# Cross-attention in split fp32: three waits at the two ends taken out, and ScalarE issuing the low query copies of every pair

## The chip, the cores and the metric

The kernel runs on one core of a Trainium2 chip. The metric is the device time of the whole program in microseconds (us), as the median of several executions. One further execution was recorded by the hardware profiler, and every duration below comes from it. The engines are named as in the profile: PE (TensorE, matrix products), PEld (its weight loads), ACT (ScalarE), DVE (VectorE), POOL (GpSimd) and SP (SyncE, which here only issues DMAs). A DMA is issued by an instruction in the queue of SP or ACT, and that queue goes on only when the issue is done; the page does not count this time as busy time of the engine. In the timelines such an issue stands under SPq or ACTq.

## The reference

Sixteen batches, 512 query rows of width 512, 77 context rows, 16 heads of width 32:

```
Q = split_heads(query @ Wq + bq)
K = split_heads(key @ Wk + bk)
V = split_heads(value @ Wv + bv)
scores = jnp.einsum('bhqd,bhkd->bhqk', Q, K) / np.sqrt(D_K).astype(np.float32)
attn = jax.nn.softmax(scores, axis=-1)
ctx = jnp.einsum('bhqk,bhkd->bhqd', attn, V)
ctx = ctx.transpose(0, 2, 1, 3).reshape(B, S, D_MODEL)
out = ctx @ Wo + bo
return _layer_norm(out + query, ln_gamma, ln_beta)
```

Key and value are both the context. All is float32.

## The kernel before

**Split operands.** A float32 product is made of three fast ones: each operand is split into a high part (rounded, by ACT) and a low part (the rest, by DVE or POOL), and high x high, high x low and low x high are summed in PSUM. So `xh`/`xl` are the query rows, `qh`/`ql` the projected queries, `ch`/`cl` the attention output, `woh`/`wol` the output weights.

**Stages.** `project_context` computes K for all batches (written to DRAM) and the first two row tiles of V. `attend` then runs 64 *slots*, one for each chunk of four heads of each batch, and four more to drain. In slot g the engines work on different chunks at once (the `LAG_` constants): PE projects the queries of chunk g into `p_q`, computes the scores of chunk g-3, multiplies probabilities with V for two chunks at a time in every odd slot, projects one 128-row tile of output (chunk number g-8) into `p_o`, and computes a first score pass `p_a` from which DVE takes row maxima. Slots go in *pairs* (2p, 2p+1), since `qh`, `ql`, the maxima `nmt` and the operand `z` of the scores are held for a pair, in two buffers.

**The operand z.** For the scores, `z` holds per head the high part of the query twice, the low part once and the row maximum, stacked on partitions. It is put together by DMAs from SBUF to SBUF: 8 copies of `qh`, 4 of `ql` (32 partitions by 1024 numbers each, one per head), 4 of `nmt`. SP issues all of them in the odd slot and the even one after it; only for the first pair and the last (`at_edge`) does ACT issue the four `ql` copies (`copy_low`), and SP the maxima right behind `qh`.

**Order.** Every engine runs its own list of instructions in program order, `slot(g)` for each g in turn (slots 16 to 55 in a hardware loop over eight slots). Waits are on semaphores. On ACT an odd slot ends with the exponentials `exp`, `ctx_high`, `mean_over_std`, `normalize`, then `split_x_high` (the high part of the query rows for five slots on) and `load_xt` (the next rows' DMA); the next even slot begins with `q_high`, which PE's `rowmax_scores` needs, then `ctx_high` and `exp`. POOL makes `xl` from `xh` (L1201) as the last step of a slot and, first thing in an even slot, two `cl` (L1220). PE's `project_out` needs the `cl` of chunk kc before it uses it, in the first tile of each batch, which falls in every fourth slot (`t == 0`, L733 to L735).

**The head.** In slots 2 to 9 the rest of V is projected in the place of `project_out`: PE writes `p_o`, DVE adds the bias (`add_bv`, L1079), ACT stores it. In slots 4 and 5 the four chunks of Wo are split by ACT (`woh`, L900) and POOL (`wol`, L1260); the raw chunks borrow buffers that DVE's `spread` and `divide` need afterwards. At the start of slot 8 ACT issues the DMAs of two residual tiles and of the rows `bo`, `ln_gamma` and `ln_beta`.

Of the kernel before, what the change touches and what calls it, by code (L numbers as in the profile page):

```python
# [26 lines left out]
P = 128  # L27
D = 512
KC = D // P
# [5 lines left out]
PAIR = 2 * NCH  # L35
# [325 lines left out]
def attend(nc, block, a, keep, kh_dram, kl_dram, v_dram, out, B, S, S2):  # L361
# [21 lines left out]
    with ExitStack() as ctx:  # L383
# [42 lines left out]
        stored = [sem(f"stored{i}") for i in range(4)]  # L426
        rows_in = sem("rows_in")
        x_last_in = [sem(f"x_last_in{t}") for t in range(QT)]
# [57 lines left out]
        def at_edge(g):  # L486

            return isinstance(g.u, int) and PAIR * g.u + g.k in (1, NG - 1)

# [36 lines left out]
        def _(sp):  # L526
# [63 lines left out]
            def slot(g):  # L590
                if g.k % 2 == 0 and g.back(2).valid(NG) and not at_edge(g.back(1)):
                    load_maxima(g.back(2))
                if g.k % NCH == 0 and g.valid(NG):
                    load_ks(g)
                if g.k % NCH == 2 and g.valid(NG):
                    load_v(g.back(2))
                if g.k % NCH == 2 and g.back(2 - NCH).valid(NG):
                    if g.back(2).is_first():
                        sp.wait_ge(kb1_zeroed, 1)
                    load_kb(g.back(2 - NCH))  # L600
                if g.k % 2 == 1 and g.back(1).valid(NG):
                    c = g.back(1)
                    i = c.k // 2 % 2
                    all_at_least(sp, (qh_ready, c.over(1, 2)), (s_summed, c.over(2, -1, HALF)))
                    for part in range(2):
                        load_z(part, i, qh)
                    if at_edge(g):
                        load_maxima(c)
                    else:
                        all_at_least(sp, (ql_ready, c.over(1, 2)))  # L610
                        load_z(2, i, ql)
                if g.back(LAG_STORE).valid(NS):
                    store(g.back(LAG_STORE))
                for half in range(2):
                    if g.back(WO_SLOTS[half] - 1).is_first():
                        load_wo(2 * half)
                        load_wo(2 * half + 1)

# [18 lines left out]
        def _(pe):  # L637
# [77 lines left out]
            def sums(g):  # L715

                pe.wait_ge(part_ready, g.over(1, 1))
                at_least(pe, rec_ready, g.over(1))
                for j in range(HC):
                    last = nc.tensor.matmul(den_single[DK * j:DK * (j + 1), :], sel[:], part[:, g.k % 2, QB * j:QB * (j + 1)],  # L720
                                            start=True, stop=True)
                last.then_inc(pv_summed, 1)
# [46 lines left out]
            def slot(g):  # L769
# [9 lines left out]
                if not g.valid(NG):  # L779
                    pe.wait_ge(cx_ready, v.over(1))  # L780
                    values(v)
# [20 lines left out]
        def _(act):  # L802
# [56 lines left out]
            def copy_low(g):  # L859

                i = g.k // 2 % 2
                act.wait_ge(ql_ready, PAIR * g.u + g.k + 1)
                for j in range(HC):
# [42 lines left out]
            def slot(g):  # L906
                s, v, m, n = g.back(LAG_SCORE), g.back(LAG_PV), g.back(LAG_NORM), g.back(LAG_SPLIT)
                w = v.back(1)
                if g.back(ROWS_SLOT).is_first():
                    act.wait_ge(v_summed, VT)  # L910
                    load_residual(Slot(0, 0))
                    load_residual(Slot(0, 1))
                    for row, src in ((bo, "bo"), (gamma, "ln_gamma"), (beta, "ln_beta")):
                        act.dma_start(row[:], a[src].partition_broadcast(P)).then_inc(rows_in, 16)
                if g.valid(NG):
                    q_high(g)
                if g.back(1).is_first():
                    copy_low(g)
# [5 lines left out]
                if m.valid(NS):  # L924
                    square(m)
                    if g.valid(NG):
                        variance(m)
                if g.back(LAG_NORM - 2).valid(NS) and not g.back(ROWS_SLOT - 1).is_first() and not g.back(ROWS_SLOT).is_first():
                    load_residual(g.back(LAG_NORM - 2))
# [11 lines left out]
                if g.is_first():  # L941
                    split_x_high(Slot(0, KC))
                if at_edge(g) and not g.back(1).is_first():
                    copy_low(g)
# [7 lines left out]
                if last_tile(g.back(-1)) == 0:  # L952
                    load_last(QT - 1)
                for kc in wo_in_slot(g):
                    split_wo_high(kc)
# [32 lines left out]
        def _(dve):  # L988
# [100 lines left out]
            def slot(g):  # L1089
                v, m = g.back(LAG_PV), g.back(LAG_NORM)  # L1090
                if m.valid(NS) and not g.valid(NG):
                    add_residual(m)
# [8 lines left out]
                if g.back(LAG_NORMALIZE).valid(NS) and not g.valid(NG):  # L1101
                    minus_mean_over_std(g.back(LAG_NORMALIZE))
                for i in v_in_slot(g.back(1)):
                    add_bv(i)
                if m.valid(NS) and g.valid(NG) and g.k % 2 == 1:
# [83 lines left out]
        def _(pool):  # L1189
# [18 lines left out]

            def scale(m):
                pool.wait_ge(normed, m.over(1, 1))  # L1210
                nc.gpsimd.tensor_tensor(rows(m), rows(m), gamma[:], ALU.mult).then_inc(scaled, 1)  # L1211
# [11 lines left out]
            def add_bo(m):  # L1223
                if m.is_first():
                    pool.wait_ge(rows_in, 48)
                pool.wait_ge(xn_in[m.k % 2], m.over(2, 1, 16))
# [128 lines left out]
```

## Time and profile before

| what | value |
|---|---|
| median of 3 executions | 609.81 us (609.68 to 613.28) |
| profiled execution | 609.58 us, of which the recorded span is 607.8 us |
| granted TensorE clock, mean | 0.992 of full speed |
| busy in the span | PE 97%, DVE 79%, POOL 73%, PEld 70%, ACT 66% |
| DMA | 129.56 MB, mean 213 GB/s |

The span is cut by the profile into what each engine did and what it waited for. Busy shares are averages over the head (about 0 to 120 us), the steady slots (to about 560 us) and the drain. A pair of slots takes 16.3 us in the steady part.

### The profile page before, as it was taken

The page shows a single profiled execution, that of the slowest core. Times are in us where ns is not written, and L with a number is a line of the kernel's source. Part 1 is how long each engine was busy: PE and PEld are TensorE (multiplying, and loading weights), DVE is VectorE, ACT ScalarE, POOL GpSimd, SP SyncE. Part 2 cuts the span into 40 slices and gives each one's busy share as a digit, 9 for nine tenths or more (in the row PEclk, how much of TensorE's full clock was granted, in tenths as well). Part 3 has the DMA queues.
Part 4 walks back from the last instruction along what each step waited for, and adds up shares of the span by engine and source line. Part 5 has one row for each costly group of instructions (what it writes and reads, how often), then busy time and mean ns, then how long its engine had stood idle before and what let it go on. Part 6 is the DMA issues. An engine that isn't in the chain of part 4 may idle for free.

```text
span 607.8 us, 11567 instructions
## 1 busy us (share of the span) xinstructions
PE 587.6 (97%) x3102; PEld 426.3 (70%) x3102; DVE 477.2 (79%) x775; ACT 401.8 (66%) x837; POOL 445.8 (73%) x396
## 2 busy tenths in 40 slices
PE   8999989999999999999999999999999999999793
PEld 6877757677777777777777777777777777777362
DVE  6535568788888888888888888888888888888776
ACT  5622553567777777777777777777777777776562
POOL 1364252377888888888889888888888888987785
PEclk9999999999999999999999999999999999999998
DMA  8868897979898898988887988898898989796513
GB/s 297 330 223 209 244 218 172 247 175 229 214 213 225 211 229 207 233 230 216 208 221 209 221 216 220 216 207 223 218 218 220 232 214 217 212 218 174 149 54 138
DMA packets 93455, 129.56 MB, mean 213 GB/s; under 512 B 50000, under 2 KB 50000, under 8 KB 93424
## 3 DMA queue, kind: packets, MB, share of 16 engines
q1 hardware_dynamic: 73888, 93.27, 61.6%
q10 hardware_dynamic: 19536, 35.92, 21.5%
q8 instruction: 14, 0.23, 0.2%
q14 instruction: 17, 0.14, 0.1%
HBM read 53.94 MB, written 24.35 MB: 129 GB/s over the span
## 4 chain that ended last, share of the span: by engine, by line
PE 91%; POOL 3%; DVE 2%; ACT 1%; ACTq 1%; issue 1%; DMA 1%; DVEq 0%; SPq 0%; POOLq 0%
PE p_q L650 28%; PE p_o L737 27%; PE p_s L688 10%; PE p_v L699 9%; PE p_a L674 6%; PE pk L323 5%; PE p_o L113 3%; PE pvv L113 1%; PE p_a L754 1%; DMA cx<-in_ctx_t 1%; POOL prob L1195 1%; PE p_q L754 0%; POOL xl L1201 0%; POOL wol L1260 0%; ACT ch L835 0%
## 5 line engine op out<-in xcount | busy, mean ns | idle before, releaser
L810 ACT ACTIVATE prob<-p_s 77x512 f32<-77x512 f32 x256 | 141.6, 591 | 82.6 <-PE p_s L688 74.3
L1070 DVE TENSOR_REDUCE nm<-p_a 128x4 f32<-128x308 f32 x256 | 117.8, 469 | 53.0 <-PE p_a L674 49.5
L1201 POOL TENSOR_TENSOR xl<-xt,xh 128x512 fp32r<-128x512 f32 x60 | 77.4, 1291 | 102.5 <-ACT xh L817 102.4
L1011 DVE TRANSPOSE_TENSOR_REDUCE part<-prob 96x64 f32<-96x2048 f32 x64 | 146.7, 2292 | 0.1
L650 PE MATMUL p_q<-xl,wqh 128*128 128x512 f32 x256 | 101.0, 395 | 0.0
L650 PE MATMUL p_q<-xh,wqh 128*128 128x512 f32 x256 | 101.0, 395 | 0.0
L650 PE MATMUL p_q<-xh,wql 128*128 128x512 f32 x256 | 100.9, 394 | 0.0
L737 PE MATMUL p_o<-woh,ch 128*128 128x512 f32 x240 | 96.1, 400 | 0.9 <-DVE y L1003 0.9
L737 PE MATMUL p_o<-wol,ch 128*128 128x512 f32 x240 | 94.7, 395 | 0.0
L737 PE MATMUL p_o<-woh,cl 128*128 128x512 f32 x240 | 94.6, 394 | 0.0
L688 PE MATMUL p_s<-z,ks 97*77 97x512 f32 x256 | 93.8, 407 | 0.4 <-ACT prob L810 0.4
L825 ACT ACTIVATE qh<-p_q,bq_col 128x512 fp32r<-128x512 f32 x64 | 44.0, 687 | 75.2 <-PE p_q L650 71.6
L1220 POOL TENSOR_TENSOR cl<-cxt,ch 128x512 fp32r<-128x512 f32 x64 | 82.4, 1302 | 14.5 <-ACT ch L835 14.5
L1227 POOL TENSOR_TENSOR xn<-xn,bo_row 128x512 f32<-128x512 f32 x60 | 77.6, 1293 | 4.7 <-DMA beta_row<-in_ln_beta 4.7
L674 PE MATMUL p_a<-kb,qh 128*128 128x308 f32 x256 | 79.3, 310 | 1.7 <-ACT qh L825 1.4
L1215 POOL TENSOR_TENSOR y<-y,beta_row 128x512 f32<-128x512 f32 x58 | 75.6, 1303 | 4.5
L1211 POOL TENSOR_TENSOR y<-y,gamma_row 128x512 f32<-128x512 f32 x58 | 75.3, 1298 | 0.0
L1062 DVE SCALAR_TENSOR_TENSOR ql<-p_q,bq_col,qh 128x512 fp32r<-128x512 f32 x64 | 47.8, 746 | 32.2 <-ACT qh L825 32.2
L699 PE MATMUL p_v<-prob,vb 77*32 77x512 f32 x512 | 62.0, 599 | 2.4 <-DVE cxt L1055 2.4
L674 PEld LDWEIGHTS p_a<-kb,qh 128*128 128x128 f32 x256 | 48.6, 190 | 21.3 <-issue 4.3
L737 PEld LDWEIGHTS p_o<-woh,ch 128*128 128x128 f32 x240 | 45.3, 189 | 16.5 <-issue 2.5
L650 PEld LDWEIGHTS p_q<-xh,wqh 128*128 128x128 f32 x256 | 48.0, 188 | 11.5
(140 smaller groups left out, 946.9 us busy)
## 6 DMA issues: line engine op xcount, KB each, us to landing
z<-qh SPq DMA_DIRECT2D x256, 128.0 KB, 3.0
z<-ql SPq DMA_DIRECT2D x120, 128.0 KB, 4.2
xn<-in_x ACTq DMA_DIRECT2D x60, 256.0 KB, 3.6
out_dram<-y SPq DMA_DIRECT2D x60, 256.0 KB, 4.1
xt<-in_x_t ACTq DMA_DIRECT2D x58, 256.0 KB, 4.3
ks<-k_high SPq DMA_DIRECT2D x32, 154.0 KB, 4.6
cx<-in_ctx_t SPq DMA_DIRECT2D x4, 616.0 KB, 5.1
k_high<-kth SPq DMA_DIRECT2D x4, 616.0 KB, 3.6
```

The lines of the kernel that those rows point to most:

```text
L650: last = nc.tensor.matmul(p_q[:], w[:, kc, P * c:P * (c + 1)], x[:, i, kc, :], start=(kc == 0 and n == 0), stop=(kc == KC - 1 and n == 2))
L674: nc.tensor.matmul(p_a[t % 2][:, 0:HC * S2], qh[:, g.k // 2 % 2, g.k % 2, P * t:P * (t + 1)], kb[g.k // NCH % 2][:, g.k % NCH, :], start=T ...
L688: nc.tensor.matmul(p_s[j % 2][0:S2, :], ks[0:KR, g.k // NCH % 2, h, :], z[0:KR, i, j, g.k % 2, :], start=True, stop=True).then_inc(s_summe ...
L699: nc.tensor.matmul(bank[DK * j:DK * (j + 1), :], vb[0:S2, g.k // NCH % 2, DK * h:DK * (h + 1)], prob[0:S2, g.k % 2, j, :], start=True, sto ...
L737: last = nc.tensor.matmul(p_o[:], x[:, i, kc, P * t:P * (t + 1)], w[:, kc, :], start=(kc == 0 and n == 0), stop=(kc == KC - 1 and n == 2))
L810: nc.scalar.activation(prob[0:S2, g.k % 2, j, :], p_s[j % 2][0:S2, :], ACT.Exp, scale=SCALE).then_inc(prob_ready, 1)
L1011: nc.vector.tensor_reduce(part[:, g.k % 2, :], prob[0:KP, g.k % 2, :, :].rearrange("p h (i r) -> p (h i) r", r=DK), AX_X, ALU.add, apply_t ...
L1070: nc.vector.tensor_reduce(nm[:, t, g.k % 2:HALF:2], p_a[t % 2][:, 0:HC * S2].rearrange("p (h k) -> p h k", k=S2), AX_X, ALU.max, negate=Tr ...
L1201: nc.gpsimd.tensor_tensor(xl[:, i, n.k % KC, :], xt[:, n.k % 2, :], xh[:, i, n.k % KC, :].bitcast(F32), ALU.subtract).then_inc(xl_ready, 1)
L1215: nc.gpsimd.tensor_tensor(rows(m), rows(m), beta[:], ALU.add).then_inc(y_done, 1)
L1220: nc.gpsimd.tensor_tensor(cl[:, i, g.k % NCH, :], cx[:, g.k % 2, :], ch[:, i, g.k % NCH, :].bitcast(F32), ALU.subtract).then_inc(cl_ready, 1)
L1227: nc.gpsimd.tensor_tensor(xn[:, m.k % 2, :], xn[:, m.k % 2, :], bo[:], ALU.add).then_inc(xb_ready, 1)
```

## The change

It has these parts.

- `at_edge` is now true in every odd slot. So ACT issues the four `ql` copies of every pair (`copy_low`, behind `normalize` and ahead of `split_x_high`), 120 DMAs that SP issued before, and SP issues the maxima of every pair right behind its `qh` copies, where it waits for DVE's `turn_maxima`, and not in the next even slot.
- DVE does `add_bv` at the start of a slot, ahead of `spread` and `divide`.
- SP loads all four chunks of Wo in slot 3 (before: two in slot 3 and two in slot 4).
- In slot 8 ACT issues one residual tile and `bo` ahead of `q_high`; the other residual tile comes in the usual place of the slot, and `ln_gamma` and `ln_beta` at its end. POOL's first `add_bo` waits for `bo` alone, and its first `scale` for the other two.
- In the drain, PE's `values` of the first single chunk waits for one `cx_ready` less, and `sums` waits for that one.

```diff
@@ attend
-        rows_in = sem("rows_in")
+        rows_in, bo_in = sem("rows_in"), sem("bo_in")
...
         def at_edge(g):
-            return isinstance(g.u, int) and PAIR * g.u + g.k in (1, NG - 1)
+            return g.k % 2 == 1
@@ sync, slot
-                for half in range(2):
-                    if g.back(WO_SLOTS[half] - 1).is_first():
-                        load_wo(2 * half)
-                        load_wo(2 * half + 1)
+                if g.back(WO_SLOTS[0] - 1).is_first():
+                    for kc in range(KC):
+                        load_wo(kc)
@@ tensor
             def sums(g):
                 pe.wait_ge(part_ready, g.over(1, 1))
+                pe.wait_ge(cx_ready, NG - LAG_PV)
...
                 if not g.valid(NG):
-                    pe.wait_ge(cx_ready, v.over(1))
+                    pe.wait_ge(cx_ready, v.over(1, -1) if v.over(1) == NG - LAG_PV else v.over(1))
                     values(v)
@@ scalar
             def copy_low(g):
                 i = g.k // 2 % 2
-                act.wait_ge(ql_ready, PAIR * g.u + g.k + 1)
+                all_at_least(act, (ql_ready, g.over(1, 1)))
...
                     load_residual(Slot(0, 0))
-                    load_residual(Slot(0, 1))
-                    for row, src in ((bo, "bo"), (gamma, "ln_gamma"), (beta, "ln_beta")):
-                        act.dma_start(row[:], a[src].partition_broadcast(P)).then_inc(rows_in, 16)
+                    act.dma_start(bo[:], a["bo"].partition_broadcast(P)).then_inc(bo_in, 16)
...
-                if g.back(1).is_first():
+                if g.valid(NG) and g.back(1).is_first():
                     copy_low(g)
...
-                if at_edge(g) and not g.back(1).is_first():
+                if g.valid(NG) and at_edge(g) and not g.back(1).is_first():
                     copy_low(g)
...
+                if g.back(ROWS_SLOT).is_first():
+                    for row, src in ((gamma, "ln_gamma"), (beta, "ln_beta")):
+                        act.dma_start(row[:], a[src].partition_broadcast(P)).then_inc(rows_in, 16)
@@ vector, slot
                 v, m = g.back(LAG_PV), g.back(LAG_NORM)
+                for i in v_in_slot(g.back(1)):
+                    add_bv(i)
...
                     minus_mean_over_std(g.back(LAG_NORMALIZE))
-                for i in v_in_slot(g.back(1)):
-                    add_bv(i)
@@ gpsimd
             def scale(m):
+                if m.is_first():
+                    pool.wait_ge(rows_in, 32)
...
                 if m.is_first():
-                    pool.wait_ge(rows_in, 48)
+                    pool.wait_ge(bo_in, 16)
```

On ACT, this is the border between an odd slot (11) and the even slot behind it (12), before. `prob<-p_s` is `exp`, `y<-y,nmr,rstd` is `normalize`, `xh<-xt` is `split_x_high`, `qh` is `q_high`.

```order
L835 CAST ch<-cxt 128x512
L855 ACTIVATE over_d<-rstd 128x1
L857 ACTIVATE nmr<-ysum,over_d 128x1
L889 ACTIVATE y<-y,nmr,rstd 128x512
L817 CAST xh<-xt 128x512
L875 DMA xt<-in_x_t 128x512
L825 ACTIVATE qh<-p_q,bq_col 128x512
```

The same place on ACT in the changed kernel.

```order
L835 CAST ch<-cxt 128x512
L855 ACTIVATE over_d<-rstd 128x1
L857 ACTIVATE nmr<-ysum,over_d 128x1
L889 ACTIVATE y<-y,nmr,rstd 128x512
L864 DMA z<-ql 32x1024 x4
L817 CAST xh<-xt 128x512
L875 DMA xt<-in_x_t 128x512
L825 ACTIVATE qh<-p_q,bq_col 128x512
```

Four DMA issues now stand between `normalize` and everything that the even slot's `q_high` comes behind.

On SP, slots 13 to 15, before: `z<-nmt` are the maxima, and stand an `out_dram` store behind the copies of `ql`.

```order
L587 DMA z<-qh 32x1024 x8
L587 DMA z<-ql 32x1024 x4
L621 DMA out_dram<-y 128x512
L582 DMA z<-nmt 1x32x32 x4
L552 DMA vb<-v_all 77x512
L533 DMA kb<-k_high 32x4x77 x4
L621 DMA out_dram<-y 128x512
L587 DMA z<-qh 32x1024 x8
```

The same slots on SP in the changed kernel.

```order
L587 DMA z<-qh 32x1024 x8
L582 DMA z<-nmt 1x32x32 x4
L620 DMA out_dram<-y 128x512
L552 DMA vb<-v_all 77x512
L533 DMA kb<-k_high 32x4x77 x4
L620 DMA out_dram<-y 128x512
L587 DMA z<-qh 32x1024 x8
```

The four `ql` copies are gone from SP, and the maxima have moved ahead of the odd slot's store.

## Rows read from the trace of the kernel before

**Rows 1.** Stretches: length, then busy us of each engine (count), PEclk, DMA share, GB/s.

```profile
301.00:560.00 259.00, 259.00 (x1400) 187.76 (x1399) 219.70 (x350) 190.19 (x410) 216.97 (x190) 1.00 0.87 216
...
333.70:350.00 16.30, 16.30 (x90) 11.76 (x89) 13.76 (x22) 12.11 (x27) 13.71 (x12) 1.00 0.92 222
```

**Rows 2.** Waits of PE, whole span: total us, times, longest us.

```profile
PE p_v L699 <- DVE cxt L1055: 2.4, 1, 2.4
```

**Rows 3.** Page, DMA issues: count, KB of each, median us from issue to landing.

```profile
z<-ql SPq DMA_DIRECT2D x120, 128.0 KB, 4.2
...
xt<-in_x_t ACTq DMA_DIRECT2D x58, 256.0 KB, 4.3
```

**Rows 4.** Timeline of SP, a steady pair, then the last pair: start, us, what.

```profile
295.32 5.04 SPq L587 DMA_DIRECT2D z<-qh  x8
300.40 2.60 SPq L587 DMA_DIRECT2D z<-ql  x4
...
562.89 2.95 SPq L582 DMA_DIRECT2D z<-nmt  x4
```

**Rows 5.** Timeline of ACT, last pair, end of slot 63.

```profile
562.62 0.81 ACT L889 ACTIVATE y<-y,nmr,rstd 128x512 f32<-128x512 f32 x1
562.62 2.77 ACTq L864 DMA_DIRECT2D z<-ql  x4
```

**Rows 6.** Timeline of ACT, border of two slots: [idle before <- what ended it].

```profile
334.32 0.82 ACT L889 ACTIVATE y<-y,nmr,rstd 128x512 f32<-128x512 f32 x1
334.67 0.35 ACTq L875 DMA_DIRECT2D xt<-in_x_t  x1
335.04 0.60 ACT L817 CAST xh<-xt 128x512 fp32r<-128x512 f32 x1
336.62 0.69 ACT L825 ACTIVATE qh<-p_q,bq_col 128x512 fp32r<-128x512 f32 x1 [0.97 <-PE p_q L650]
337.20 0.61 ACT L835 CAST ch<-cxt 128x512 fp32r<-128x512 f32 x1
337.71 1.08 ACT L810 ACTIVATE prob<-p_s 77x512 f32<-77x512 f32 x2
```

**Rows 7.** The chain that ended last, same even slot: start, us, what.

```profile
337.67 0.17 PE p_a L674
...
338.53 0.29 PE p_s L688
...
338.96 0.69 PE p_o L737 x3
...
340.03 0.69 PE p_o L737 x3
```

**Rows 8.** Timeline of POOL, same border of slots.

```profile
335.73 1.30 POOL L1201 TENSOR_TENSOR xl<-xt,xh 128x512 fp32r<-128x512 f32 x1 [2.37 <-ACT xh L817]
336.98 2.56 POOL L1220 TENSOR_TENSOR cl<-cxt,ch 128x512 fp32r<-128x512 f32 x2
```

**Rows 9.** Timeline of ACT in the head, slot 4 and the start of slot 8.

```profile
69.31 0.69 ACT L825 ACTIVATE qh<-p_q,bq_col 128x512 fp32r<-128x512 f32 x1 [2.66 <-PE p_q L650]
...
103.68 1.60 ACTq L870 DMA_DIRECT2D xn<-in_x  x2
...
106.74 0.86 ACTq L914 DMA_DIRECT2D beta_row<-in_ln_beta  x1
```

**Rows 10.** Timeline of DVE in slot 6, then of PE in slots 6 and 8.

```profile
87.34 0.69 DVE L1055 TENSOR_TENSOR cxt<-p_v,rden 128x512 f32<-128x512 f32 x1 [3.14 <-POOL wol L1260]
...
88.69 0.50 PE L113 MATMUL p_o<-wvh,ch 128*128 128x512 f32 x1 [2.69 <-DVE y L1079]
...
108.46 0.41 PE L674 MATMUL p_a<-kb,qh 128*128 128x308 f32 x1 [1.01 <-ACT qh L825]
```

**Rows 11.** Stretches behind those two waits of PE, columns as in the first group.

```profile
89.80:93.00 3.20, 3.20 (x9) 2.36 (x9) 1.74 (x3) 0.59 (x1) 0.26 (x1) 0.50 0.93 225
...
108.50:111.00 2.50, 2.50 (x12) 1.86 (x13) 1.98 (x4) 1.99 (x4) 1.31 (x1) 1.00 1.05 254
```

More of the change, by code:

```diff
@@ L927, in slot @@
                         variance(m)
-                if g.back(LAG_NORM - 2).valid(NS) and not g.back(ROWS_SLOT - 1).is_first() and not g.back(ROWS_SLOT).is_first():
+                if g.back(LAG_NORM - 2).valid(NS) and not g.back(ROWS_SLOT - 1).is_first():
                     load_residual(g.back(LAG_NORM - 2))
```

## The prediction

> **What bounds the kernel now.** I looked first at a long steady stretch cut by engine. From 301 to 560 us PE is busy for all of the 259.00 us, at a granted clock of 1.00, which is the 2.4 GHz level [rows 1]. So in the steady part nothing can be gained on any queue but PE's, and what counts is whether another engine begins to make PE wait. Next come the waits of PE over the whole span: nine rows in all, none of which names a DMA; the two longest are one of 2.69 us in the head [rows 10] and one of 2.4 us in the drain [rows 2]. The third view is the border between an odd and an even slot, on ACT, PE and POOL side by side [rows 6 to 8], since the four DMA issues are put there. A pair of slots takes 16.30 us [rows 1].
>
> **What the moved copies cost on ACT.** Of the 32 pairs 30 are touched: 120 copies leave SP [rows 3] and come to ACT, four in each odd slot. The trace of before shows the same four copies on ACT at the same place, in the last pair. There the issue begins when `normalize` begins and takes 2.77 us, while `normalize` itself takes 0.81 us [rows 5]. SP was issuing maxima in the same 3 us [rows 4, 5], which is what the changed order does in every pair, so this is the right price. It is also near SP's own for such copies: 2.60 us for four `ql`, 5.04 us for eight `qh`, 2.52 us for four [rows 4]. A plain load takes 0.35 us to issue [rows 6].
>
> Now the border, with N as the start of `normalize` (334.32 in [rows 6]). Before: `xh` at N+0.72, `qh` at N+2.30, and ACT stood idle for 0.97 us ahead of `qh`, waiting for PE's projection. PE's `p_a`, which needs `qh`, started at N+3.35, and `qh` was done at N+2.99, so 0.3 us were spare. After: the copies hold ACT's queue from N to about N+2.8, `xh` starts at N+2.85 and takes about 0.55; the `xt` issue of 0.35 us fits beside it; then come the register steps and waits of `q_high`. I put `qh` at N+3.5, 1.2 us later. What follows on PE [rows 7]:
> - `p_a` can start when `qh` is done, N+3.5+0.69+0.04 = N+4.23, against N+3.35: 0.9 us late.
> - The third score product `p_s`, at N+4.21 before, needs the first `exp` of this slot. `exp` starts 1.09 us behind `qh` (through `ch`) and half of the 1.08 us pair is the first one; with a hand-over that is N+3.5+1.09+0.6 = N+5.2: 1.0 us late.
> - POOL's `xl` starts 0.69 us after `xh` [rows 6, 8], now at N+3.54, and the two `cl` stand behind it: done at N+3.54+1.25+1.28 = N+6.07 and at N+7.35. In the first tile of a batch, PE's third and fourth chunk of `p_o` wait for these. They ran at N+4.64 and N+5.71 [rows 7]; with the 1.0 us already lost PE reaches the third at N+5.64 and waits to N+6.1, reaches the fourth 1.07 us later, N+7.17, and waits to N+7.4: 1.7 us late in all.
>
> So a pair costs 1.0 us, and one whose even slot has the first tile of a batch 1.7 us. Nothing gives that back in the odd slot, because PE has no idle time there [rows 1]: the next `normalize` follows PE's last score product of the odd slot, which is as late as PE is. The odd slots 11 to 61 have `normalize` in front and an even slot behind: 26 pairs, half of each kind. 13 x 1.0 + 13 x 1.7 = 35.1 us. In slots 59 and 61 there are no query rows left to split, so `xh` and `xl` are missing and `qh` comes about 0.55 us earlier; I take off 1.6 us for the two together. That makes **33.5 us**.
>
> **What is free.** POOL takes the later `xl` out of its 2.37 us of idle [rows 8]; it is busy for 13.71 us of a pair of 16.30 [rows 1], and the pair becomes longer; without that cover the two `cl` would grow later from pair to pair. On SP the maxima come earlier by one place; behind their wait for `turn_maxima` now stand the odd slot's store and the next slot's loads of K, which move by at most the 2.95 us of the four maxima [rows 4]. PE waits for none of them, so I take 0. `ql` lands about 4.2 us after its issue [rows 3], near N+7; the scores of that pair begin in the next odd slot, later than a slot of some 7 us and a projection, so some 4 us are spare. The 2.60 us taken off SP per pair are worth 0, since PE waited for no copy of `z`.
>
> **Head and drain.** In slot 6 PE waited 2.69 us for `add_bv`, which stood on DVE behind `divide`, which waited 3.14 us for the last `wol` [rows 10]. `add_bv` now goes first and PE gets past this. But the copies of slot 5 stand on ACT ahead of the split of Wo's last two chunks, so `wol`, `divide`, `ch` and the slot's first `exp` all come later, and PE's third score product waits for that `exp` instead. Bounds: a gain of 2.69 us plus the 1.6 us lost to the low clock behind it (3.20 us at 0.50, the 1.2 GHz level [rows 11]), and a loss of 1 us; I take 0. In slot 8 ACT loses, ahead of `q_high`, the issue of a residual tile (half of 1.60), of `ln_beta` (0.86) and of `ln_gamma`, which has the same shape and which I take at 0.65 [rows 9], 2.3 us in all, and gets four copies, 2.77 us: PE's wait of 1.01 us there [rows 10] stays, and grows by 0.3 at most. In slot 3 the copies fill an idle of 2.66 us [rows 9]. In the drain the wait of 2.4 us [rows 2] goes, but the `exp` that PE needs next stands on ACT behind the copies of slot 63, which are there before and after [rows 5]; bounds 0 and -2.4, taken 0. Head and drain together: 0, between -6 and +1.
>
> **The sum.** 609.58 us, the profiled execution, which is 0.23 us from the median of the runs, plus 33.5 is **643 us**.
>
> **Rivals.** *Faster: the issue is cheap on ACT, or covered.* If a copy cost what a plain load does, 0.35 us, four would take 1.4 us, `xh` would start at N+1.5, and `qh` would still wait for PE. It turns at 1.8 us for the four, 0.45 each: beyond that `qh` is later than its 2.30 and the 0.2 us that the third score product has to spare. Then the head's gain is kept too, 2.69 us in slot 6 and about 0.9 in slot 8 (2.3 less 1.4): 606 us. For it speaks only the row of the plain load; all rows of copies of this shape, on both queues, show 0.63 to 0.69 us. Chance 0.05. The Trainium skill, Perfetto Trace Analysis, DMA Optimizations, speaks for this side: where an engine's queue is full of DMA issue, spreading the DMAs over other engines that can issue them may help. SP does spend 5.04 + 2.60 + 2.95 us of a pair on `z` [rows 4], but by rows 1 the rule's condition, that issuing is what binds, isn't met.
>
> *Partly hidden.* If the `cl` wait didn't bind and the copies cost SP's 2.52 us, a pair would lose 0.75: 26 x 0.75 = 20 us, 629 us. The low end of the range.
>
> *Loads behind the copies.* On ACT's DMA queue `xt` now stands behind 512 KB of `ql`. It is issued near N+3 and wanted by the next `split_x_high`, a slot of 7.2 us and the stall of 1.0 later than N+0.72, near N+8.9: 5.9 us, where it took 4.3 [rows 3]. If it took 4.3 + 4.2, ACT would wait 2.6 us, of which about 0.9 falls into its idle ahead of `qh`; with 1 us of the rest on PE in each pair it would be 643 + 26 = 669 us. Against it: the copies are issued over 2.8 us, and most have landed by then. Chance 0.07.
>
> *The clock falls.* After the 2.69 us wait the granted clock was 0.50 for 3.20 us [rows 11], which cost 1.6 us. If every pair's stall did this: 26 x 1.6 = 42 us more, 685 us. Against it: after the wait of 1.01 us in slot 8 the clock stayed at 1.00 [rows 10, 11], and here the pieces of a stall are 1.0 us at most. Chance 0.03. The Trainium skill, TensorE: Matmul & The Clock Gate, Part 1, says that an idle PE is put back to half its rate; rows 11 show both outcomes.
>
> **How the numbers follow.** Forecast, 643 us, with its neighbours from 628 to 658: 0.81. Low end: copies at 2.52 us (26 x 0.25 = 6.5 less) and no `cl` term (12 x 0.7 = 8.4 less). High end: copies at SP's price for maxima, 2.95 (26 x 0.18 = 5 more), and 0.35 us of register steps ahead of the copies in the loop, which is what ACT took from `normalize` to the `xt` issue (26 x 0.35 = 9 more). Faster, 606: 0.05. Loads: 0.07. Clock: 0.03. Anything between 603.5 and 616, as a stall that is mostly absorbed: 0.04. 628 to 658 leaves out 0.19. A measurement of this kernel tells about 1%, 6 us, from no change: faster 0.05, same 0.03, slower 0.92.
>
> **What would show it.** Right: in the timeline of ACT each odd slot has four L864 issues of 2.5 to 3 us behind `normalize`, with an idle put down to "issue" behind them; among the waits of PE `p_a <- ACT qh` stands first with some 20 us, with smaller ones for `prob` and for `cl`; PE's busy share in the middle falls from 100% to 92 to 94%; a pair takes 17.3 to 18 us. Wrong: copies of 0.4 us on ACT, PE without idle time in the middle, or ACT waiting for `xt`.

## The result, and the profile after

The changed kernel takes 667.43 us (median of 4 executions, 666.93 to 670.06) against 609.87 us for the kernel before: a ratio of 1.0937, 95% interval 1.0907 to 1.0968. The forecast was 643 us, in a range of 628 to 658. The direction was right and the size too small: 57.6 us of span were lost (665.4 against 607.8), where the sum had 33.5.

First the three parts of the two traces, from the starts of `qh`. Slot 10 ends the head, slot 62 begins the drain.

| stretch | before | after | difference |
|---|---|---|---|
| start to `qh` of slot 10 | 124.32 | 127.01 | +2.7 |
| `qh` of slot 10 to `qh` of slot 62 (26 pairs) | 424.25 | 478.46 | +54.2 |
| `qh` of slot 62 to the end | 59.22 | 59.94 | +0.7 |

So nearly all of the loss lies in the steady pairs. The head of the page of the changed kernel: PE's share has fallen from 97% to 91%, on the same instructions.

```profile
PE 608.2 (91%) x3102; PEld 431.6 (65%) x3102; DVE 478.8 (72%) x775; ACT 405.5 (61%) x837; POOL 444.7 (67%) x396
...
z<-ql ACTq DMA_DIRECT2D x128, 128.0 KB, 2.8
...
xt<-in_x_t ACTq DMA_DIRECT2D x58, 256.0 KB, 3.0
```

The DMA rows answer to [rows 3]: both transfers now land sooner after their issue (2.8 us against 4.2, 3.0 against 4.3), so neither became the bound. The waits of the changed kernel, as in [rows 2] (total, times, longest):

```profile
PE p_a L673 <- ACT qh L825: 38.8, 30, 2.6
...
ACT xh L817 <- DMA xt<-in_x_t: 4.8, 3, 2.5
...
PE p_s L687 <- ACT prob L810: 2.8, 2, 2.6
...
PE p_o L737 <- POOL cl L1223: 1.8, 7, 0.3
```

PE waits for `qh` 30 times; 26 of these waits are one in each pair from slot 12 to slot 62. ACT's waits for the DMA of `xt` are no more than before (there 4.9 us, 3 times). In the steady part ([rows 1] showed PE without any idle time) a long stretch reads now as follows, and behind it stand three neighbouring stretches of 2 us at one of the waits, and the part of them with the low clock:

```profile
300.00:540.00 240.00, 221.04 (x1146) 156.75 (x1144) 179.35 (x287) 159.23 (x338) 176.82 (x157) 0.98 0.77 192
...
514.00:516.00 2.00, 1.52 (x6) 0.90 (x6) 1.22 (x3) 2.00 (x5) 2.00 (x3) 1.00 0.94 288
516.00:518.00 2.00, 1.85 (x5) 1.40 (x6) 2.00 (x2) 1.30 (x4) 2.00 (x2) 0.59 1.27 209
518.00:520.00 2.00, 2.00 (x8) 1.68 (x7) 1.13 (x3) 1.89 (x5) 1.92 (x3) 0.56 0.56 134
...
516.40:519.70 3.30, 3.30 (x10) 2.54 (x10) 2.57 (x2) 2.49 (x7) 3.22 (x3) 0.50 0.97 174
```

PE is busy for 92.1% of the 240 us, and the granted clock is 0.98, not 1.00: in places it goes down to 0.50, the 1.2 GHz level, as the last row shows.

The border on ACT, the one of [rows 6] (slots 35 and 36); N, the start of `normalize`, is 361.29 here and was 334.32.

```profile
361.29 0.81 ACT L889 ACTIVATE y<-y,nmr,rstd 128x512 f32<-128x512 f32 x1
361.29 2.77 ACTq L864 DMA_DIRECT2D z<-ql  x4
364.22 0.62 ACT L817 CAST xh<-xt 128x512 fp32r<-128x512 f32 x1 [2.12 <-PE p_q L649]
364.45 0.35 ACTq L875 DMA_DIRECT2D xt<-in_x_t  x1
364.99 0.69 ACT L825 ACTIVATE qh<-p_q,bq_col 128x512 fp32r<-128x512 f32 x1
```

`xh` now starts at N+2.93 and `qh` at N+3.70, against N+2.30. (The 2.12 us of idle time is put down to a product of PE, but `xh` does not read `p_q` here any more than in [rows 6]; what lies in that time is the row of the four copies.) The same border on PE, whose rows answer to [rows 7]:

```profile
364.24 0.40 PE L737 MATMUL p_o<-woh,cl 128*128 128x512 f32 x1
365.81 0.40 PE L673 MATMUL p_a<-kb,qh 128*128 128x308 f32 x1 [1.16 <-ACT qh L825]
...
366.75 0.44 PE L687 MATMUL p_s<-z,ks 97*77 97x512 f32 x1
...
367.59 0.48 PE L737 MATMUL p_o<-woh,ch 128*128 128x512 f32 x1 [0.26 <-POOL cl L1223]
...
368.85 0.47 PE L737 MATMUL p_o<-woh,ch 128*128 128x512 f32 x1
```

The idle of 1.16 us understates the loss, since a product's modelled duration (0.40) overlaps the next start: in this timeline products of this shape start 0.23 us after each other, and here two starts lie 1.57 us apart, so 1.34 us went by. And POOL, as in [rows 8]:

```profile
364.92 1.27 POOL L1202 TENSOR_TENSOR xl<-xt,xh 128x512 fp32r<-128x512 f32 x1 [3.95 <-ACT xh L817]
366.15 2.56 POOL L1223 TENSOR_TENSOR cl<-cxt,ch 128x512 fp32r<-128x512 f32 x2
```

`xl` starts at N+3.63 and the second `cl` is done at N+7.42. For the working below, three rows of the kernel **before** in the same slot, from PE's timeline (in [rows 7] these products were read from the chain of waits):

```profile
337.50 0.34 PE L674 MATMUL p_a<-kb,qh 128*128 128x308 f32 x1
...
338.37 0.45 PE L688 MATMUL p_s<-z,ks 97*77 97x512 f32 x1
...
339.87 0.39 PE L737 MATMUL p_o<-woh,ch 128*128 128x512 f32 x1
```

In the head, ACT at the end of slot 3 and the start of slot 4 of the changed kernel, the place of the first row of [rows 9]:

```profile
65.49 3.25 ACTq L864 DMA_DIRECT2D z<-ql  x4
...
68.91 1.15 ACTq L875 DMA_DIRECT2D xt<-in_x_t  x1
70.10 1.05 ACTq L895 DMA_DIRECT2D v_all<-y  x1
71.28 0.69 ACT L825 ACTIVATE qh<-p_q,bq_col 128x512 fp32r<-128x512 f32 x1 [1.82 <-POOL xl L1202]
```

And PE's three long waits in the head, in slots 4, 6 and 8, of which the last two answer to [rows 10]:

```profile
72.02 0.41 PE L673 MATMUL p_a<-kb,qh 128*128 128x308 f32 x1 [1.65 <-ACT qh L825]
...
92.71 0.45 PE L687 MATMUL p_s<-z,ks 97*77 97x512 f32 x1 [2.58 <-ACT prob L810]
...
111.51 0.41 PE L673 MATMUL p_a<-kb,qh 128*128 128x308 f32 x1 [1.61 <-ACT qh L825]
```

The wait for `add_bv` in slot 6 is gone, and one of the same size for `exp` stands in its place.

### The profile page after: what moved, and what is told of

Its sections match the earlier page's. It is cut to its first block, busy times and chain, and to the rows that moved or that the text cites. A ratio compares the mean times of both kernels' runs of the same rounds, so it can differ in the third digit from the quotient of the medians.

```text
span 665.4 us, 11568 instructions
## 1 busy us (share of the span) xinstructions
PE 608.2 (91%) x3102; PEld 431.6 (65%) x3102; DVE 478.8 (72%) x775; ACT 405.5 (61%) x837; POOL 444.7 (67%) x396
## 4 chain that ended last, share of the span: by engine, by line
PE 36%; POOL 31%; issue 19%; ACTq 6%; ACT 5%; DVE 2%; DMA 1%; POOLq 0%; DVEq 0%; SPq 0%
PE p_o L737 10%; PE p_q L649 7%; POOL cl L1223 7%; POOL y L1214 6%; POOL xn L1230 6%; POOL xl L1202 5%; PE p_v L698 4%; ACTq L864 4%; PE pk L323 4%; PE p_s L687 4%; POOL y L1218 4%; POOL rstd L1208 2%; PE p_o L113 2%; PE p_a L673 2%; ACT ch L835 2%
## 5 line engine op out<-in xcount | busy, mean ns | idle before, releaser
L673 PE MATMUL p_a<-kb,qh 128*128 128x308 f32 x256 | 82.9, 324 | 39.1 <-ACT qh L825 38.8
L737 PE MATMUL p_o<-woh,ch 128*128 128x512 f32 x240 | 99.4, 414 | 1.9 <-POOL cl L1223 1.8
L687 PE MATMUL p_s<-z,ks 97*77 97x512 f32 x256 | 96.4, 417 | 2.8 <-ACT prob L810 2.8
L737 PE MATMUL p_o<-woh,cl 128*128 128x512 f32 x240 | 97.6, 407 | 0.0
L737 PE MATMUL p_o<-wol,ch 128*128 128x512 f32 x240 | 97.5, 406 | 0.0
L673 PEld LDWEIGHTS p_a<-kb,qh 128*128 128x128 f32 x256 | 50.0, 195 | 66.7 <-issue 39.6
L817 ACT CAST xh<-xt 128x512 fp32r<-128x512 f32 x60 | 36.8, 613 | 69.7 <-issue 45.5
```

The source lines that it names most:

```text
L673: nc.tensor.matmul(p_a[t % 2][:, 0:HC * S2], qh[:, g.k // 2 % 2, g.k % 2, P * t:P * (t + 1)], kb[g.k // NCH % 2][:, g.k % NCH, :], start=T ...
L687: nc.tensor.matmul(p_s[j % 2][0:S2, :], ks[0:KR, g.k // NCH % 2, h, :], z[0:KR, i, j, g.k % 2, :], start=True, stop=True).then_inc(s_summe ...
L737: last = nc.tensor.matmul(p_o[:], x[:, i, kc, P * t:P * (t + 1)], w[:, kc, :], start=(kc == 0 and n == 0), stop=(kc == KC - 1 and n == 2))
```

## The experiments

Theory at the start: the loss is ACT's queue being held ahead of `qh` (offset of `qh` from N), plus a term for `cl` behind a late `xl`, plus the clock. Rivals were that SP's new order, the transfers themselves or the edits at the ends cost something. Ratios are to the kernel before on the same chip, with 95% intervals; "steady" is the stretch from slot 10 to slot 62, 424.25 us before, and like every row it is read from one profiled execution of a run. The loop's borders are the even slots at which a round of the hardware loop begins, or the loop ends: 16, 24, 32, 40, 48 and 56.

**1. The edits at the ends alone.** The changed kernel with the old `at_edge`.

```diff
         def at_edge(g):
-            return g.k % 2 == 1
+            return isinstance(g.u, int) and PAIR * g.u + g.k in (1, NG - 1)
```

> The changed kernel with SP issuing the low copies again, in the order of before; the edits to head and drain stay. Theory (ScalarE's queue is held by the four issues, nothing else costs): no pair is late, and the head keeps its gain in slots 6 and 8, so 605 to 609.6 us. Rival (the head edits themselves cost what the head lost, 2.7 us): 611 to 614 us. If the ends were the cause of the whole loss: near 667 us.

Measured: 610.45 us against 611.23, ratio 0.9993 (0.9969 to 1.0017): 0.85 us above what the theory had, and below the rival. In its profiled execution slot 10 comes 3.7 us earlier (120.61 against 124.32), steady is 424.25 to the hundredth, and the drain is 0.7 longer. PE's waits there:

```profile
PE p_s L687 <- ACT prob L810: 1.9, 2, 1.7
PE p_v L720 <- DVE part L1012: 1.9, 1, 1.9
```

The 2.69 us of slot 6 became 1.7, and the low clock behind it and the 1.01 us of slot 8 are gone; the 2.4 us of the drain [rows 2] became 1.9 us at the next product, `sums`. The median shows no gain that is clear of noise. None of the 57 us comes from here.

**2. The moved copies alone**, in the kernel before (`at_edge` true in every odd slot, with SP's maxima and the changed waits around `copy_low`, left out below; the ends as they were).

```diff
         def at_edge(g):
-            return isinstance(g.u, int) and PAIR * g.u + g.k in (1, NG - 1)
+            return g.k % 2 == 1
...
```

> The kernel before with only the copies moved to ScalarE and the maxima right behind the high copies. Theory: all of the loss is here, 664 to 670 us. Rival (the two parts make each other worse): under 655 us.

Measured: 672.3 us, ratio 1.0998 (1.0937 to 1.1058), 2.3 us above the theory's range; steady 477.29 (+53.0), head +10.7. The loss belongs to the copies. In the head they cost 10.7 us without the other edits and 6.4 with them (127.01 against the 120.61 of run 1).

**3. Copies behind the split and the load.** As changed, `copy_low` moved behind `split_x_high` and `load_xt`.

```diff
-                if g.valid(NG) and at_edge(g) and not g.back(1).is_first():
-                    copy_low(g)
...
                 if g.back(LAG_LOAD_X).valid(NG):
                     load_xt(g.back(LAG_LOAD_X))
+                if g.valid(NG) and at_edge(g) and not g.back(1).is_first():
+                    copy_low(g)
```

> The changed kernel with the four issues behind the split of the query rows and the load of the next ones, still ahead of the next slot's qh. Theory: xh and xl come on time, so PE's wait for cl (0.7 us in 13 pairs) goes and with it the longest stalls, after which the clock fell; qh stays as late as it is: 645 to 655 us, granted clock above 0.98. Rival (the late qh alone makes the loss, cl and clock follow from it): 662 to 668 us.

Measured: 653.53 us, ratio 1.0707 (1.0662 to 1.0753), as the theory had it. Its ACT at such a border, ahead of slot 38:

```profile
374.33 0.82 ACT L889 ACTIVATE y<-y,nmr,rstd 128x512 f32<-128x512 f32 x1
375.01 0.77 ACTq L864 DMA_DIRECT2D z<-ql  x1
375.05 0.60 ACT L817 CAST xh<-xt 128x512 fp32r<-128x512 f32 x1
375.82 2.10 ACTq L864 DMA_DIRECT2D z<-ql  x3
378.04 0.69 ACT L825 ACTIVATE qh<-p_q,bq_col 128x512 fp32r<-128x512 f32 x1 [2.38 <-issue]
```

`xh` is back at N+0.72 and `qh` is still at N+3.71. Away from loop borders ordinary pairs take 17.7 us, and so do those with the first tile of a batch, which took 18.43 in the changed kernel: the 0.7 us for `cl` is gone and the rest is not. So the two terms are separate, as in the sum.

**4. PE kept busy while it waits.** As changed, with six products of 128x308 ahead of the wait for `qh` in the even slots from 12 on; what they write is overwritten.

```diff
+                    if g.k % 2 == 0 and g.back(12 - 1).valid(NG):
+                        at_least(pe, max_ready, g.over(1, -1, QT) + t + 3)
+                        for _ in range(6):
+                            nc.tensor.matmul(p_a[0][:, 0:HC * S2], wqh[:, 0, 0:P], woh[:, 0, 0:HC * S2], start=True, stop=True)
                     pe.wait_ge(qh_ready, g.over(1, 1))
```

> The changed kernel with six products of 128x308 put on PE in every even slot from 12 on, ahead of its wait for qh; their result is overwritten, nothing else changes. They take about 0.84 us of a stall of 1.3 us. Theory (some 10 us of the loss is the granted clock that falls in some even slots): the clock stays near 0.99 and the time falls to 655 to 660 us. Rival (the low clock costs little): 665 to 669 us. If the filling runs past the stall: over 669 us.

Measured: 662.32 us, ratio 1.086 (1.0813 to 1.0907), 2 us above the expectation. Its steady stretch, to be read beside that of the changed kernel:

```profile
300.00:540.00 240.00, 233.49 (x1259) 168.88 (x1252) 182.96 (x294) 161.83 (x345) 181.86 (x160) 1.00 0.80 196
```

The clock is back at 1.00. The pairs of 17.73 and 18.43 us are as they were, the longer ones of 19.4 to 19.8 are gone, and steady is 470.91: 7.5 us less, in spite of one pair in the last slots in which `qh` came 1.7 us late. So that much, or a little more, was the clock, and the rest is the wait itself.

**5 and 6. Two copies on ACT, then three**; SP issues the others.

```diff
-                for j in range(HC):
+                edge = isinstance(g.u, int) and PAIR * g.u + g.k in (1, NG - 1)
+                for j in range(HC if edge else 2):
```

(3 in the second), and SP's `load_z(2, i, ql, range(2, HC))` ahead of its maxima.

> The changed kernel with two of the four low copies of a pair on ScalarE (first and last pair: four) and two on SP, ahead of the maxima. Theory (ScalarE has no more than what it waited for PE, about 1.4 us, ahead of the even slot's qh; what goes beyond is lost in full): two issues take 1.4 us, qh is where it was, only cl is some tenths late in 13 pairs: 607 to 615 us. Rival (the loss goes with the number of copies): 636 to 642 us.

> The same with three of the four on ScalarE. Theory: 2.1 us, so qh is 0.7 us late in 26 pairs and cl 0.3 us more in 13: 628 to 638 us. Rival (in proportion): 650 to 656 us.

Measured: two copies 620.61 us, ratio 1.0176 (1.0141 to 1.0211); three 641.29 us, 1.0498 (1.0449 to 1.0547). Both miss: two cost more than the theory had (607 to 615) and less than the rival had, three 3 us more than the theory's 628 to 638. ACT with two copies, ahead of slot 36 as in [rows 6]:

```profile
339.02 0.81 ACT L895 ACTIVATE y<-y,nmr,rstd 128x512 f32<-128x512 f32 x1
339.03 1.26 ACTq L870 DMA_DIRECT2D z<-ql  x2
340.44 0.62 ACT L822 CAST xh<-xt 128x512 fp32r<-128x512 f32 x1 [0.61 <-issue]
...
341.32 0.69 ACT L830 ACTIVATE qh<-p_q,bq_col 128x512 fp32r<-128x512 f32 x1 [0.26 <-PE p_q L654]
```

`qh` is at N+2.30 as before and still waits 0.26 us, by the row for PE's projection, but `xh` comes 0.70 us later than in [rows 6], and with that the pair has the whole `cl` term: first-tile pairs take 17.0 us against 16.24. I had taken that term to grow with the copies; it is whole with two. At the loop's borders `qh` is late with two copies too (by 0.3 to 1.0 us).

**7. SP's order alone.** All copies on SP, the maxima right behind them in the odd slot, the ends as changed: the edit of run 1, and besides it:

```diff
-                if g.k % 2 == 0 and g.back(2).valid(NG) and not at_edge(g.back(1)):
-                    load_maxima(g.back(2))
...
                         load_z(2, i, ql)
+                        load_maxima(c)
```

> The changed kernel with all low copies on SP and the maxima issued right behind them in the odd slot: SP's new order without ScalarE's part. Theory: PE waits for none of it, so as with the ends alone, 606 to 612 us. Rival (SP's wait for the maxima, with the stores behind it, costs): 615 us or more.

Measured: 608.84 us against 610.76, ratio 0.9972 (0.9951 to 0.9992), as the theory had it; steady 424.25. SP's order costs nothing in the steady part, and the median shows no cost. In the head it is not settled: slot 10 comes at 123.66 in the profiled execution, 3.0 us later than in run 1. PE waits 1.92 us in slot 5 for nothing that the profile names (0.73 us in run 1), and the clock falls; runs 10 and 12 have such a wait there too (1.15 and 1.56 us), the changed kernel has not.

**8. ACT held without a DMA.** The kernel before, with eleven one-column scalings that nobody reads, each waiting for the one before, in the odd slots 11 to 61 behind `normalize`; the copies stay on SP.

```diff
...
+                if g.valid(NG - 1) and g.k % 2 == 1 and g.back(11).valid(NG):
+                    for r in range(11):
+                        nc.scalar.mul(idle[:], keep["eps"][:], 1.0).then_inc(idle_done, 1)
+                        act.wait_ge(idle_done, g.over(2, -5, 11) + r + 1)
```

> The kernel before, no DMA moved, but with ScalarE held for about 2.8 us at the place of the copies in the odd slots 11 to 61: eleven scalings of one column, each waiting for the one before; nothing reads them. Theory (it is the time in ScalarE's queue, not the traffic): 26 pairs lose 1.4 us, half of them 0.7 us more, and some the clock: 645 to 665 us. Rival (the DMAs' traffic on ScalarE's queue makes the loss): under 620 us.

Measured: 698.04 us, ratio 1.1448 (1.1409 to 1.1487), more than either theory had. Away from the loop's borders it does in kind what the theory says. Ordinary pairs, counted from `qh` to the next `qh`, take 18.18 us, with that next `qh` at N+4.15; first-tile pairs take 18.76, with it at N+4.04. But at the four borders of the loop's rounds something else appears, the `xt` issue and then nothing on ACT for 6.68 us. Here are ACT's rows of an ordinary pair, of such a border, and the DMA packets of kind "instruction" that fall into it (253.1 to 259.7 us):

```profile
361.73 0.69 ACT L826 ACTIVATE qh<-p_q,bq_col 128x512 fp32r<-128x512 f32 x1
...
375.75 0.81 ACT L890 ACTIVATE y<-y,nmr,rstd 128x512 f32<-128x512 f32 x1
...
379.90 0.69 ACT L826 ACTIVATE qh<-p_q,bq_col 128x512 fp32r<-128x512 f32 x1
...
252.63 0.34 ACTq L876 DMA_DIRECT2D xt<-in_x_t  x1
259.71 0.69 ACT L826 ACTIVATE qh<-p_q,bq_col 128x512 fp32r<-128x512 f32 x1 [6.68 <-issue]
...
q14 instruction: 2, 0.02, 0.9%
```

The pairs that end at such a border take 24.5 to 24.7 us, four times about 6 us more, and the low clock follows them. Besides, ACT is held longer than by the copies, so that `qh` comes 0.45 us later than in the changed kernel. That is what the time has above the expectation. No row of ACT stands in those 6.68 us, but two instruction packets of 8 KB on queue 14 fall into each of the four, and none from 262 to 294 us, behind the first. By the pages this run has 38 packets on that queue and the kernel before 17, none of them from 236.5 to 518 us. So instructions being loaded again at the border, ACT's by the place of the gap, is the likely reason. No run tried it.

**9 and 10. The head alone, and with SP's order.** Run 1 with the drain's waits put back; then with SP's order of run 7 besides. The diff is against run 1.

```diff
-                pe.wait_ge(cx_ready, NG - LAG_PV)
...
-                    pe.wait_ge(cx_ready, v.over(1, -1) if v.over(1) == NG - LAG_PV else v.over(1))
+                    pe.wait_ge(cx_ready, v.over(1))
```

> The kernel before with the edits of the head alone (bias of V first on VectorE, Wo loaded in one slot, two row loads later); the drain and all low copies as before. Theory: the head gains 3.7 us in the trace and the drain loses nothing: 605 to 608 us, ratio 0.990 to 0.996. Rival (the gain is given back): ratio 0.998 to 1.002.

> The same with SP issuing the maxima right behind the low copies in the odd slot. Theory: SP's order is worth nothing in the steady part, so the same as the head alone within 1 us, if the head takes no harm from the loads of Wo coming later on SP: 605 to 609 us. Rival (the new order is worth something): under 604 us.

Measured: 607.61 us against 611.27, ratio 0.9958 (0.9935 to 0.998), and 608.52 us, 0.9965 (0.9942 to 0.9989), both as the theory had it. Slot 10 comes 3.8 us earlier in run 9. Its median is the lowest of the study, 0.4% below the kernel before; its interval overlaps those of runs 1, 7, 10 and 12.

**11. Two copies, behind the split and the load**, the edits of runs 3 and 5 together.

> Two of the four low copies on ScalarE, issued behind the split of the query rows and the load of the next ones. Theory (qh has about 1.4 us to spare against the copies, cl some tenths): neither is late, a pair takes 16.3 us as before and the time is 606 to 613 us. Rival (each issue on ScalarE costs something wherever it stands): 618 to 622 us, as with two copies ahead of the split.

Measured: 615.79 us, ratio 1.0071 (1.0039 to 1.0103), between theory and rival, so both miss. Away from loop borders both kinds of pair take 16.25 to 16.44 us, at most 0.1 us more than before. Steady is 6.4 us longer, most of it at the loop's borders, where `qh` is 0.3 to 1.1 us late.

**12. All four copies on ACT, in the even slot.** From slot 11 on ACT issues them behind the first two `exp` of the even slot, not behind `normalize` of the odd one. SP puts the maxima right behind its copies and issues the low copies of the four pairs before slot 11 that are not the first, so 104 of the 120 moved copies are on ACT here.

```diff
+        def by_act(g):
+            return g.k % 2 == 1 and g.back(11).valid(NG)
...
+                if g.valid(NG) and by_act(g.back(1)):
+                    copy_low(g.back(1))
...
```

> All four low copies of the pairs from slot 11 on are issued by ScalarE, but in the middle of the next even slot, behind its first two exponentials; SP puts the maxima right behind the high copies there, and issues the low copies of the pairs before. Theory (there the last two exponentials are late, which nothing on PE needs before the next slot's scores, and the next qh has more than 2 us to spare on PE): a pair takes 16.2 to 16.6 us, 606 to 615 us, against 667 for the same instructions at the end of the odd slot. Rival (2.8 us of ScalarE's queue per pair cost the same anywhere): over 640 us. If the copies land too late for the scores: 620 to 635 us.

Measured: 609.19 us against 611.27, ratio 0.9974 (0.9953 to 0.9994), steady 424.57, as the theory had it. The issues take as long as at the other place, 2.90 us of ACT's queue, where nothing on PE waits for what comes behind them:

```profile
335.02 0.69 ACT L826 ACTIVATE qh<-p_q,bq_col 128x512 fp32r<-128x512 f32 x1 [0.96 <-PE p_q L650]
335.40 0.53 ACTq L865 DMA_DIRECT2D z<-ql  x1
...
335.97 0.94 ACTq L865 DMA_DIRECT2D z<-ql  x1
...
336.94 1.43 ACTq L865 DMA_DIRECT2D z<-ql  x2
338.41 0.73 ACT L842 ACTIVATE xn<-y,ysum 128x512 f32<-128x512 f32 x1 [1.22 <-issue]
```

ACT stands for 1.22 us here too, ahead of `xn`, and PE is busy for the whole of 300 to 540 us, as before. The same four copies a pair in the steady slots, on the same queue: 478.46 us of steady in the one place, 424.57 in the other.

## Why the prediction was right in direction and too small

**What holds.** The copies cost what was forecast, 2.75 to 2.87 us in 22 of the 26 pairs (3.0 to 4.05 in the others, ahead of slots 16, 18, 24 and 40). `p_a` waits for `qh` once a pair (38.8 us in all where some 20 were forecast), PE's share in the middle is 92.1% (forecast 92 to 94). The second `cl` was put at N+7.35 and is done at N+7.42, and its 0.7 us in first-tile pairs came out as 18.43 less 17.73. SP's order is free in the steady part (run 7). *The issue is cheap* and *partly hidden* fell with the 2.77 us and the `cl` term; *loads behind the copies* fell with `xt` landing in 3.0 us and ACT waiting for it 4.8 us in all, no more than the 4.9 of before.

**The failing step: what a pair loses.** The forecast let `qh` come 1.2 us later, took 0.2 to 0.3 us of that as spare, and lost 1.0. The runs show a simple rule instead. Count a pair from the `qh` of its even slot to the `qh` of the next one, away from the loop's borders. From its `qh` to the next `normalize`, N, an ordinary pair takes 14.03 us (16.33 less 2.30 before; 17.73 less 3.70 after), whatever comes ahead of it, and the offset of the next `qh` from N comes on top:

| kernel | next `qh` behind N, ordinary pair | plus 14.03 | ordinary pair measured | first-tile pair measured |
|---|---|---|---|---|
| before | 2.30 | 16.33 | 16.33 | 16.24 |
| two copies | 2.30 to 2.38 | 16.33 to 16.41 | 16.32 to 16.43 | 17.0 |
| three copies | 2.96 | 16.99 | 17.0 | 17.7 |
| changed | 3.70 | 17.73 | 17.73 | 18.43 |
| ACT held, no DMA | 4.15 | 18.18 | 18.18 | 18.76 |

Nothing is spare: each 0.1 us by which `qh` is late is lost by the pair. The reason stands in PE's rows. The third score product follows `qh` by 1.75 us before (338.37 less 336.62) and by 1.76 after (366.75 less 364.99): `exp` behind `qh` already released it. The forecast took its start from the chain of waits, 338.53 [rows 7], where a step begins only at the modelled end of the product ahead of it; the timeline has 338.37, so 0.16 us of the spare was the view's. The same holds for `p_a`, which the chain has at 337.67 and the timeline at 337.50: the 0.3 us that were read as spare there were 0.2 with the hand-over in it, and `p_a` came 1.34 us late, not 0.9. Besides, `qh` comes at N+3.70, not N+3.5, because it starts 0.77 us behind `xh` (0.65 was assumed), which is itself 0.1 us later. Together an ordinary pair loses 1.40 us, not 1.0, and a first-tile pair 2.19, not 1.7: in slot 36 the first product of the fourth `p_o` chunk is 2.01 us late against N (N+7.56 against N+5.55), where the forecast put it at N+7.4 and took the chain's N+5.71 for the old place.

In sum 13 x 1.40 + 13 x 2.19 = 46.7; the last pairs, which have no `xh`, lose 1.5 less (forecast 1.6): 45.2 us, where the same terms of the forecast gave 33.5. So the cost and the wait were right in kind, and the term for what a pair loses was sized too small.

**The clock.** It was a rival at 0.03, in the form that every pair falls; the reason against it was that the pieces of a stall are 1.0 us at most. They are 1.0 to 2.6 us in slots 12 to 60, and in five of the 26 pairs the granted clock fell. Cut into stretches of 2 us, each of the five places loses 1.7 us of full-speed time (from 516 to 520 us: 2 x 0.41 + 2 x 0.44), 8.5 us in all. That is most of the 9.0 us that steady lost beyond the 45.2 (the other 0.5 us is not assigned), and it agrees with run 4, where PE was kept busy and the loss went. The length of one wait does not say when it falls: behind the wait below, 2.63 us, the clock stayed, and behind 1.27 us for `qh` (to 514.4 us) and 0.27 us for `cl` (to 516.1 us) it fell.

```profile
183.04 0.40 PE L673 MATMUL p_a<-kb,qh 128*128 128x308 f32 x1 [2.63 <-ACT qh L825]
...
183.00:187.00 4.00, 3.96 (x17) 2.85 (x18) 3.48 (x4) 3.60 (x10) 3.95 (x4) 1.00 1.15 236
```

All five lie in first-tile pairs (slots 24, 40, 48, 52 and 56), where `cl` is late too. So do the five falls of run 2 (slots 16, 32, 40, 44 and 48); in run 3, where `cl` is on time, the clock fell in one pair, and with two or three copies in none. But most first-tile pairs with the same two waits kept the clock (`qh` 1.16 and `cl` 0.26 us in slots 36 and 44 of the changed kernel), and in run 2 slot 44 had it fall. What decides is open.

**The head.** Forecast 0, measured +2.7: the other edits give 3.7 to 3.8 back (runs 1 and 9), within the bounds that were named, but the copies take 6.4, for which the forecast had 1.3 as the most. Most of the 6.4 are PE's waits that run 1 has not or has shorter (1.65, 0.49 and 1.61 us for `qh` in slots 4, 6 and 8, 0.9 us for `exp` in slot 6) and 1.7 us for a low clock behind the last of slot 6. With the drain the ends lose 3.4 us, outside the forecast's -6 to +1. Two of its statements failed. "In slot 3 the copies fill an idle of 2.66 us": behind them the `xt` issue and the store of `v_all` took 1.15 and 1.05 us instead of 0.33 and 0.50, ACT's queue was held from 65.49 to 71.15, and PE waited 1.65 us. And in slot 8 PE's wait grew from 1.01 to 1.61 us, by 0.6 where 0.3 was the most. In slot 6 the wait changed its name only, as was said. **The drain**: the wait removed came back as 1.89 us at `sums`, and the end is 0.7 us later; forecast 0. Behind that wait the granted clock was 0.50 (625.7 to 632.3 us), where before it stayed at 1.00 behind the wait of 2.4 us (565 to 572 us); in run 9, with the old waits, it was 0.50 there too (560.9 to 567.4 us), and the drain took 60.64 us. So the 0.7 us can't be put down to the drain's edit.

The account: 45.2 (pairs) + 8.5 (clock) + 0.5 (not assigned) + 2.7 (head) + 0.7 (drain) = 57.6 us, the difference of the spans. Of the 24.1 us that the forecast lacks, 11.7 are the size of the pair's term, 8.5 the clock, which it put at nothing in its sum, and 3.4 the ends.

**What holds ACT.** Run 8 gives the same rule with no DMA moved, run 12 the same steady copies without a loss. So it is the time for which ACT's queue is held ahead of `qh`, shown from both sides, and neither the transfers nor their bandwidth. The Trainium skill, DMA: Bandwidth & Descriptors, Issuing engines are not separate DMA queues, says that starting DMAs from several engines saves only the sequencer's time for it, which is usually small relative to the DMA. Here it is 0.69 us beside 2.8 us from issue to landing, a quarter. PE waited for no copy of `z` in the steady part while SP issued them ([rows 1], run 7), so there was nothing to save on SP, and on ACT the place made it dear.

## What to carry to other kernels

In these traces a DMA issue holds its engine's queue for its full time (the four copies 2.8 us, of which only the 0.8 us of the `normalize` ahead of them still runs beside them), so when issues move to an engine that also computes, look for the first instruction behind them whose result the bounding engine waits for: here the same four issues a pair cost 54 us of the steady part or nothing, by their place in the slot. Before counting a slack, read the start of the waiting instruction in its engine's own timeline, not in the chain, and check whether it follows its releaser as closely as it ever could; if it does, there is no slack. A stall that recurs in each round can also bring the clock down in some rounds, so a forecast by waits alone can be too low.

## What was not expected of the hardware

- The time of one issue is not fixed: a load of `xt` took 0.33 us to issue at the end of slot 3 before, and 1.15 us behind four copies. In the steady pairs it took 0.35 us behind the same four copies (364.45), so the copies ahead of it don't explain that alone. Of the steady pairs of the changed kernel, the two with the longest issue of the copies (4.05 us ahead of slot 16, 3.60 ahead of slot 40) are the only ones in which an instruction packet of 16 KB ran on queue 8 during it. Whether it is the cause was not tried.
- At the borders of the hardware loop's rounds ACT loses time: 6.68 us in run 8, where two instruction packets fall into each gap, and 0.5 to 1.4 us of extra `qh` delay in the changed kernel (N+4.2 to N+5.1 against N+3.70), of which the copies' own issue explains a part in three slots (4.05, 3.10 and 3.60 us ahead of slots 16, 24 and 40). At slots 32 and 48 no row and no instruction packet explains it.
- The name beside an idle time can be that of a bystander: `xh`'s 2.12 us stand under PE's `p_q`, while the four copies are issued in that time.
